# Self-attention in a decoder layer: ScalarE instead of SyncE issues the transfers that move value rows to their sequences

## The reference

```python
q = einsum('bse,ehd->bshd', x, wq)      # k and v likewise; x is the layer-normed input
qn = rms_norm(q, q_scale)               # kn likewise
scores = einsum('bqhd,bkhd->bhqk', qn, kn)
attn = softmax(scores, axis=-1)
out = einsum('bhqk,bkhd->bqhd', attn, v)
x = x + einsum('bqhd,hde->bqe', out, wo)
```

## Time and profile before

| | |
|---|---|
| median of 3 runs | 2619.14 us (2618.99 to 2619.47) |
| the profiled execution | 2618.98 us, span of its instructions 2617.2 us |
| busy, share of the span | PE 95%, PEld 51%, DVE 59%, ACT 51%, POOL 33% |
| mean granted TensorE clock | 0.979 of full speed |
| self-attention | from the start to about 1275 us |

### The profile page before, as it was taken

How to read it: one execution, slowest core, us unless ns; L and a number is a source line. 1 busy time by engine, 2 the same in 40 slices (tenths; PEclk the granted TensorE clock), 3 DMA queues, 4 the chain that set the end, 5 groups by cost and what they waited for, 6 DMA issues and landing times.

```text
span 2617.2 us, 47837 instructions
## 1 busy us (share of the span) xinstructions
PE 2477.4 (95%) x16390; PEld 1334.0 (51%) x16390; DVE 1545.2 (59%) x3589; ACT 1343.3 (51%) x4098; POOL 866.8 (33%) x801
## 2 busy tenths in 40 slices
PE   6999999999999999999769999999999999999998
PEld 3455455555554555445344464464464465465466
DVE  7777756666666666667355555554645645645634
ACT  4555555555555555555354454454554554454433
POOL 3333333333333333324123323323323322423412
PEclk9999999999999999999869999999999999999999
DMA  5677777776777668797320001001001001000000
GB/s 154 156 176 167 155 159 153 172 170 145 157 171 157 155 154 186 168 187 166 107 77 10 16 2 37 16 2 37 15 4 37 7 12 37 1 17 24 7 17 8
DMA packets 455401, 235.37 MB, mean 90 GB/s; under 512 B 389096, under 2 KB 391784, under 8 KB 455144
## 3 DMA queue, kind: packets, MB, share of 16 engines
q1 hardware_dynamic: 455144, 232.08, 38.3%
HBM read 78.66 MB, written 32.77 MB: 43 GB/s over the span
## 4 chain that ended last, share of the span: by engine, by line
PE 82%; DVE 7%; ACT 4%; issue 3%; POOL 1%; DMA 1%; SPq 1%; DVEq 0%; POOLq 0%; ACTq 0%
PE ps L1380 22%; PE ps L1381 21%; PE ps L1382 21%; PE ps L1513 3%; PE ps L1514 2%; PE ps L1515 2%; ACT mem L887 2%; PE ps L1624 2%; PE ps L1523 1%; PE ps L1527 1%; PE ps L1525 1%; PE ps L1566 1%; PE ps L1612 1%; PE ps L1586 1%; PE ps L1554 1%
## 5 line engine op out<-in xcount | busy, mean ns | idle before, releaser
L1380 PE MATMUL ps<-mem 128*128 128x512 f16 (+6 forms) x3924 | 1204.4, 326 | 59.5 <-issue 24.6
L1381 PE MATMUL ps<-mem 128*128 128x512 f16 (+6 forms) x3924 | 1217.5, 325 | 0.0
L1382 PE MATMUL ps<-mem 128*128 128x512 f16 (+6 forms) x3924 | 1201.1, 325 | 0.0
L1380 PEld LDWEIGHTS ps<-mem 128*128 128x128 f16 (+3 forms) x3924 | 407.6, 104 | 380.8 <-issue 75.8
L1382 PEld LDWEIGHTS ps<-mem 128*128 128x128 f16 (+3 forms) x3924 | 408.7, 104 | 311.7 <-issue 9.3
L1381 PEld LDWEIGHTS ps<-mem 128*128 128x128 f16 (+3 forms) x3924 | 410.4, 105 | 300.3 <-issue 9.6
L699 POOL TENSOR_TENSOR mem<-mem 128x500 f32<-128x500 f32 (+1 forms) x231 | 268.1, 1160 | 360.2 <-ACT mem L949 207.5
L649 POOL TENSOR_TENSOR mem<-mem 128x8 f32<-128x8 f32 x100 | 163.7, 1637 | 518.3 <-DVE mem L1021 518.3
L795 ACT ACTIVATE mem<-ps,mem 100x100 f32<-100x100 f32 x512 | 169.2, 345 | 223.4 <-DVE mem L1051 222.3
L1336 DVE TENSOR_TENSOR mem<-mem 128x500 f16<-128x500 f32 (+1 forms) x231 | 144.5, 649 | 188.7 <-ACT mem L931 184.7
L661 POOL TENSOR_TENSOR mem<-mem 100x400 f16<-100x400 f32 x128 | 158.4, 1237 | 175.7 <-ACT mem L805 175.7
(11 more groups left out here) (121 smaller groups left out, 3132.5 us busy)
## 6 DMA issues: line engine op xcount, KB each, us to landing
x<-mem SPq DMA_DIRECT2D x100, 256.0 KB, 2.9
mem<-x SPq DMA_DIRECT2D x75, 256.0 KB, 3.5
mem<-in_x SPq DMA_DIRECT2D x50, 256.0 KB, 3.6
mem<-x SPq DMA_DIRECT2D x12, 1000.0 KB
mem<-mem SPq DMA_DIRECT2D x32, 200.0 KB
out<-mem SPq DMA_DIRECT2D x6, 1000.0 KB
mem<-in_wq SPq DMA_DIRECT2D x16, 256.0 KB, 4.0
mem<-in_wk SPq DMA_DIRECT2D x16, 256.0 KB, 4.2
```

The lines of the kernel that those rows point to most:

```text
L1380: pe.matmul(out_ap, ah, bh, start=(i == 0), stop=False)
L1381: pe.matmul(out_ap, ah, bl, start=False, stop=False)
L1382: mm = pe.matmul(out_ap, al, bh, start=False, stop=(i == len(pairs) - 1))
```

## The change

`place_values` moves from SyncE's program to ScalarE's. SyncE called it at the head of its step n for the tiles `valued_at(n - 1)`; ScalarE calls it at the end of its step n, for the same tiles, after the squares. The waits and the transfers themselves are the same, and SyncE's other work keeps its order.

```diff
@@ SyncE
-            def place_values(u):
-
-                sp.wait_ge(s["vlo"], u + 1)
-                if u >= 2:
-                    sp.wait_ge(s[f"vb{u % 2}"], placed(u - 2))
-                for n, row, to, count in value_runs(u):
-                    if n >= 3:
-                        sp.wait_ge(s["o"], n - 2)
-                    sp.dma_start(v[to:to + count, n % 3, :, :], vt[row:row + count, u % 2, :, :]
-                                 ).then_inc(s[f"vb{u % 2}"], 16)
-
             for n in range(FIRST_STEP, STEPS + 3):
-                for u in valued_at(n - 1):
-                    place_values(u)
                 for w in summed_at(n - 1):
                     store_sum(w)
@@ ScalarE
+            def place_values(u):
+
+                act.wait_ge(s["vlo"], u + 1)
+                if u >= 2:
+                    act.wait_ge(s[f"vb{u % 2}"], placed(u - 2))
+                for n, row, to, count in value_runs(u):
+                    if n >= 3:
+                        act.wait_ge(s["o"], n - 2)
+                    act.dma_start(v[to:to + count, n % 3, :, :], vt[row:row + count, u % 2, :, :]
+                                 ).then_inc(s[f"vb{u % 2}"], 16)
+
@@ ScalarE, the end of its step
                 for u in projected_at(n):
                     squares(u)
+                for u in valued_at(n - 1):
+                    place_values(u)
```

## The result

| | before | after |
|---|---|---|
| median of 4 runs each | 2619.3 us (2618.99 to 2625.26) | 2717.71 us (2711.26 to 2721.63) |
| span of the profiled execution | 2617.2 us | 2719.8 us |
| ratio of the times | | 1.0366 (95%: 1.0351 to 1.0381) |

The change costs 98 us, eleven times what I forecast, and the time lies 68 us above the range. The sign was right and the size was not.

A forecast was written before the change was run, and what follows sets the result against it. Only TensorE's idle time in self-attention was taken to count, some 50 us in play. Terms +8.7 + 0.8 + 2.1 + 2.1 + 3.4 - 6.2 gave +10.9 us, taken as 9: 2628 us, range 2609 to 2650.

The forecast's parts named there:

- (b): TensorE's value mixes in self-attention: values land late, 2.9 us after issue, at 11 three-piece steps; 14.2 us, against 12.1 before.
- My own sentence on the rule: One descriptor generator serves both issuing engines under a lock, so ScalarE's moves would stand behind SyncE's coinciding transposes.
- The upper bound of 5.5 us: Landing of a value move: from a second value issue near 1132.5 to its mix at 1138.01; lower bound zero.
- For tiles with two pieces I counted one step and 2.1 us: One more late-value step, with 1.54 us of room before its mix: 0.77 + 2.9 - 1.54 = 2.1 us.
- (c): Exponentials on ScalarE start late where the transposes behind them are just in time: three steps, 3.4 us.
- (a): First head group: late take_o_hi (L822) delays VectorE and the scaled queries (L1029): six waits, 8.7 us, plus 0.8.
- What SyncE gains: Self-attention pauses removed by freeing SyncE of 224 issues: 12.1 us at three-piece steps and 6.2 elsewhere, 18.3 in all.
- the 12.1 us that I called removable: Nine TensorE pauses after three-piece steps, where SyncE's hold delays transposes; removable in all but one of 1.29 us.
- The list of what would make me wrong: Signs: ScalarE issue far from 0.77 us, pieces landing under 2.4 us, L1029 waits unchanged, or L539 longer.
- Rivals 1 and 3: The first: issue hidden on ScalarE, SyncE's relief stays, 2602 to 2615, chance 0.20; the other: nothing measurable, chance 0.21.
- rival 3: Losses and gains of 10 to 20 us cancel; with landing 2.1 and (a) 1.0 a time, near +2, 2621; chance 0.21.
- Rival 2: ScalarE's moves queue behind SyncE's transposes: +21 us, 2649, or near 2700 with an L539 besides; chance 0.14.

## Why the prediction was wrong

**The step that failed: the landing of the moves, term (b).** "I take 2.9, about two thirds of a transpose's, since on ScalarE's queue no transpose stands ahead of a move." The queue was the wrong thing to look at. Some 3 us is what a move takes where it goes out ahead of the transposes (3.1 before, 3.1 with the transposes held, 3.4 ahead of the squares). Beside them it takes 4.8, and in the tiles with three pieces, which the term is made of, 5.5, though no transpose stands in ScalarE's queue. My own sentence on the rule had noted that ScalarE's first free moment and SyncE's L558 coincide; I gave that to a rival at 0.14 and let my own sum go on as if transfers in flight didn't share anything. The upper bound of 5.5 us that I had from a row was what these tiles showed.

**The count of steps, too.** For tiles with three pieces it was nearly right: 11 steps forecast, 13 waits measured. Their size was not: 14.2 / 11 = 1.3 us forecast, 45.7 / 13 = 3.5 measured. The landing gives 5.5 - 2.9 = 2.6 of that difference, and issues that start about 0.4 us earlier than I had put them take some of it back (the last one a median 1.71 us after the squares' start, where I had 0.60 + 1.55). For tiles with two pieces I counted one step and 2.1 us, and it was 9 waits and 29.9 us. So 16.3 us for late values became 75.6. A sum over steps near an edge has to be made at both ends of the bound, not only at the value taken.

**No term for the clock.** Extra pauses cost a second time when TensorE then runs at 1.2 GHz for some us. This was 33.2 us of busy time, a third of the loss. It comes and goes with the waits: 2510.6 us in after, 2478.8 with the pieces ahead of the squares. A change forecast to add many pauses of some us needs this term.

**(c), the late exponentials, was too small, and (a) hit its number partly by luck.** L1029's waits rose by 10.7 us where I had 9.5. The mechanism of (a) is there: with the issues alone on ScalarE they rise by 5.5, in five waits that are each 0.6 to 1.3 us longer, where I had 1.45 for six. But they also rise by 8.1 with the moves late and ScalarE free, which (a) knew nothing of. ScalarE's issuing time by itself costs 28 to 33 us, and (a) and (c) with 12.9 us were to cover it. "issue" pauses in that run are up by 11.5 us, which I read as transposes of probabilities that come late (I had counted three steps), and 11.6 us is added busy time.

**What SyncE gains was right in some rows and overrated in time.** "issue" pauses fell by 9.6 us and L1066's by 7.2, in sum 16.8 where I had 18.3. In after, though, pauses before scores also fall because TensorE has just been stopped before a mix, so this match proves little. Where only the third piece leaves its place at the head of SyncE's step, "issue" pauses fall by 3.9 to 7.5 us, and the time by 2.3 to 4.6. So the 12.1 us that I called removable by relief of SyncE alone were mostly not.

**What stood.** The price of an issue on ScalarE (0.766 us against 0.774). The new wait for `o` costs nothing (0.9995). The list of what would make me wrong ended with the right suspicion, "or L539 longer than before, since ScalarE's moves now share its moment": its median landing is 5.1 us against 4.5, and L547's 4.6 against 3.4.

**The rivals.** Rivals 1 and 3 are out. (By its own numbers rival 3 comes to 10.9 - 2.7 - 8.8 - 0.8 = -1.4 us and not near +2; this changes nothing.) Rival 2 is the one that came nearest, 2649 to near 2700, by another mechanism. It had the issues queue for a lock: by the Trainium skill, Perfetto Trace Analysis, section Per-instruction lifecycle, one descriptor generator is locked for exclusive use and an issue's recorded time begins with the wait for it. In the step shown L810 and L547 start 0.04 us apart, L547 takes 1.23 us like its median and the moves 0.77, 0.78 and 0.57. Over self-attention 175 of the 224 issues on ScalarE overlap one of SyncE's; they take 0.75 us in the mean, and so do the other 49. L539's issues did grow, from a median 2.26 to 2.98 us, but not for a lock: with the 224 issues in the same place and 8 bytes in a row they take 2.22. No waiting for each other is to be seen in the issues; the lateness is in the data. So this case's trace doesn't show the lock between these two engines. For the data the Trainium skill, DMA: Bandwidth & Descriptors, section Issuing engines are not separate DMA queues, has the rule that I should have weighed: transfers from all issuing engines run on the same 16 DMA engines and interleave. The landing times of both kinds agree with it. The same section says that several issuing engines save only the sequencer's time, usually small relative to the transfer. Here that time, some 172 us in all, was 28 to 33 us of the kernel's once it stood on ScalarE.

**What stays open.** By the runs with added transfers, the excess of after splits into some 28 to 33 us for ScalarE's time and, as the rest, some 65 for late values, both with their share of the clock. The runs don't add up to this exactly: pieces ahead of the squares keep all 224 issues on ScalarE and cost 19 us, as part of the issuing then falls into a gap. Whether transposes and moves share DMA engines evenly, or a transpose blocks an engine for longer than its bytes say, was not tried: no run changed the size of a move or of a transpose. Nor does a run tell which of the two transposes slows the moves.

## What to carry to other kernels

Moving a transfer to another engine's queue changes when it goes out, and what else is in flight then; look for that, not only for the queue's own time. Put an issue ahead of an instruction that waits anyway rather than behind it: here that was worth 78 us, partly because the moves also got ahead of the transposes. And move only those transfers that hold the old queue, here 24 of 224. Where a mix, a bank or a buffer is needed within a few us of the landing, work the sum at both ends of the landing time, and add the clock for each new pause of several us.

## What the runs showed of the hardware

- A tile's moves (at most 100 rows of 2 KB each) took 3.1 us to land where they went out ahead of the transposes and 4.8 where they went out beside them from another queue (5.5 for tiles with three pieces). From one queue, between the two transposes, they took 3.4. Transposes of probabilities took 3.4 before and 4.6 beside the moves. Which queue issued it made no difference in the duration of an issue (0.77 us on either).
- After a pause of 4.32 us the 128x512 matmuls started 0.43 us apart for some 3.4 us and then 0.22 again. Over the kernel this added 33 us to the busy time of the same 16390 matmuls.
- Two engines that issued at the same time didn't lengthen each other's plain issues: 0.75 us in the mean on ScalarE, for the 175 that overlapped one of SyncE's and for the 49 that didn't.
- Taking away nearly all bytes of 224 transfers of 512 bytes a row saved some 5 of their 33 us: here the price of such a transfer was its issue.
- A wait for the engine's own issuing appears in the waits as one for a transfer ("<- DMA mem<-mem", 97 us before `take_o_hi`). Whether it is one shows only in the timeline, where it ends with the last issue.
